# Twelve instead of eight tiles turned by VectorE, a ring of eight row slots, and loads reordered on SyncE's queue

## The chip, the cores and the metric

The kernel runs on one core of a Trainium2 chip. The metric is the time of one execution in device microseconds; the number given for the kernel before is the median of three runs.

## The reference, cut to what matters

2048 tokens of 512 values go through two layers. The first gives each token to one of four experts by its token id; the expert's matrix is `ctx_2048[e]`, used three times. The second is a gated MLP with 1408 inner columns, whose weights are -1, 0 or 1.

```python
def _L0_xattn_ref(hidden_states, token_ids, Wg, Wu, Wd):
    tid = jnp.clip(token_ids, 0, VOCAB - 1)
    expert_ids = jnp.minimum(tid // tokens_per_expert, E - 1)
    out = jnp.zeros_like(hidden_states)
    for e in range(E):
        g = jax.nn.silu(jnp.einsum('bsd,fd->bsf', hidden_states, Wg[e]))
        u = jnp.einsum('bsd,fd->bsf', hidden_states, Wu[e])
        y = jnp.einsum('bsf,df->bsd', g * u, Wd[e])
        out = jnp.where((expert_ids == e)[..., None], y, out)
    return out
...
    g = jnp.einsum('th,ih->ti', xf, gate_w) * gate_s
    u = jnp.einsum('th,ih->ti', xf, up_w) * up_s
    hdn = jax.nn.silu(g) * u
    out = jnp.einsum('ti,hi->th', hdn, down_w) * down_s
...
x = x + jnp.tanh(g_xattn[0]) * _L0_xattn_ref(_layernorm(x, axis=-1), itok, ctx_2048, ctx_2048, ctx_2048)
x = x + jnp.tanh(g_ffn[0]) * _L0_ffn_ref(_layernorm(x, axis=-1), gate_w, up_w, down_w, gate_s, up_s, down_s)
```

## The kernel before

**Stages.** First a routing stage sorts the tokens by expert into 19 tiles of 128 rows (16 full tiles of tokens, and up to three more because each expert starts a new tile). Then 19 steps of the expert layer, one for each tile (k = 0 to 18). Then four blocks of the MLP, each of four tiles. The order on every engine is written out by hand; engines meet through semaphores only.

**A step on TensorE** (`expert_step(k)`) is: `first_product(k)`, 12 matmuls of 128x512; while k+1 is under `ON_PE`, `turn_x(k + 1)`, four 128x128 transposes of the normalised rows of the next tile; `second_product(k - 1)`, again 12 matmuls; `turn_h(k)`, four transposes. `second_product(k - 1)` waits until `update(k - 2)` has emptied its PSUM bank (`rows_ready`) and for `h_lo(k - 1)`; `turn_h(k)` waits for `hidden(k)`.

**The rows of x.** GpSimd gathers a tile's rows from HBM into a ring slot (`gather`) and, after `update` on VectorE has added the expert's result, scatters them to HBM (`store`). The ring has `RING = 6` slots in the buffer `rows`, which has four more for the first MLP block. `stats(m)` is three VectorE instructions (bn_stats, bn_aggr, and the variance plus eps); GpSimd makes of them 1/std (`inverse_std`), and `norm(m)` writes the normalised rows into the one buffer `xn`.

**Turning x.** Of tiles 0 to 10 x is turned by TensorE. For tiles 11 to 18 SyncE writes `xn` to HBM (`turned_rows<-xn`), waits for it to land, and reads it back in another order (`xq<-turned_rows`): that is `turn_rows(n)` for tile n + 11. A VectorE transpose of 32x32 blocks (`turn`) then finishes it, and `turned_hi` (ScalarE) and `turned_lo` (VectorE) split it into the two parts that the matmuls take. The MLP blocks 1 to 3 turn their tiles in the same way.

**SyncE's queue** carries, in one order, the MLP's gate and up weights (`weight_row`, 8 rows of 704 KB), rows of the down weights only to be looked at (`check_row`, 11 of 256 KB), the pairs of write and read of `turn_rows`, and `load_half`, which brings two finished tiles (528 KB) from HBM back for MLP block 0. SyncE executes in order: a wait ahead of one of them holds all that follow. `first_stats(t)`, t = 0 to 3, are the statistics of these four tiles on VectorE; `first_stats(0)` waits for the first half and `first_stats(2)` for the second.

**Where the numbers are.** In the profile's lines: L1178 is either product of a step, L1157 `turn_x`, L1193 `turn_h`, L763 to L770 `stats`, L784 `norm`, L790 to L794 `first_stats`, L808 and L848 the low part of x, L822 `hidden`, L826 `h_lo`, L833 `update`, L842 the VectorE transpose, L535 `silu`, L339 and L344 write and read of `turn_rows`, L327 `load_half`, L306 `check_row`, L299 `weight_row`, L1283 and L1290 the MLP's matmuls.

Of the kernel before, what the change touches and what calls it, by code (L numbers as in the profile page):

```python
# [13 lines left out]
F32 = mybir.dt.float32  # L14
# [9 lines left out]
P = 128  # L24
# [15 lines left out]
RING = 6  # L40
ROWS = RING + BLOCK
# [13 lines left out]
ON_PE = 11  # L55
# [11 lines left out]
def ring_slot(k):  # L67

    return (k + 4) % RING


def row_slot(b, t):

    return t + RING * ((b + 1) % 2)

# [6 lines left out]
def build(nc, x, ids, ctxT, g_x, g_f, guT, dwT, gate_s, up_s, down_s, out):  # L82
# [7 lines left out]
    with ExitStack() as ctx:  # L90
# [12 lines left out]
        work = sb("work", [P, CTX_WORDS + XBUF_WORDS], F32R)  # L103
# [42 lines left out]
        xt0 = nc.alloc_sbuf_tensor_at("xt0", [P, D], F32, offset=work_base + (CTX_WORDS + 3 * D) * 4)  # L146
        wraw = nc.alloc_sbuf_tensor_at("wraw", [P, 2 * KC, 2, INTER], F32, offset=wgu_base)
# [65 lines left out]
        def token_of(first, last):  # L213

            return rows[:, first:last, D:D + 1].bitcast(U32)
# [30 lines left out]
        def quarter_rows(expert=False):  # L246

            return xq0[:, :] if expert else rows[:, RING - 2, 0:D]

        def turned_x(expert=False):  # L250

            return xt0[:, :] if expert else rows[:, RING - 1, 0:D]

# [3 lines left out]
        def down_w(c, s):  # L257
# [3 lines left out]
            row_landed w_hi w_lo down_hi down_lo  stored rows_a rows_b  # L261
# [9 lines left out]
        down_landed = [sem(f"down_landed{n}") for n in range(4)]  # L271
        last_stored = [sem(f"last_stored{t}") for t in range(BLOCK)]

# [7 lines left out]
        def _(sp):  # L281
# [36 lines left out]
            check_row(4)  # L318
            weight_row(4)
            sp.wait_ge(S["ctx_lo"], len(ON_VECTOR))  # L320
            sp.wait_ge(S["pool_ctx_lo"], len(ON_POOL))
            def load_half(b, half_):
                t = BLOCK * b + 2 * half_
                at = row_slot(b, 2 * half_)
                if b == 0:
                    sp.wait_ge(S["stored"], 16 * (t + 2 + EXPERTS - 1))
# [3 lines left out]
            for r in range(5, 2 * KC):  # L330
                check_row(r)
                weight_row(r)
            load_half(0, 0)
            check_row(8)

            def turn_rows(n):
# [3 lines left out]
                             xn[:, :].rearrange("p (i c) -> p i c", i=QUADS)).then_inc(S["xn_out"], 16)  # L340
# [5 lines left out]

            turn_rows(0)
            load_half(0, 1)
            check_row(9)
            turn_rows(1)  # L350
            check_row(10)
            for n in range(2, AHEAD):
                turn_rows(n)
            for c in range(IC):
                if c < 4:
                    sp.wait_ge(S["stored"], 16 * (TILES + c))
                else:
                    sp.wait_ge(S["down_lo"], c - 3)
# [14 lines left out]
        def _(pool):  # L373
# [30 lines left out]
            def gather(k):  # L404
                at = ring_slot(k)
                pool.indirect_dma_start(  # L406
                    rows[:, at, 0:D], None, x, bass.IndirectOffsetOnAxis(ap=gidx[:, k:k + 1], axis=0))\
                    .then_inc(slot_landed[at], 16)

            def store(k):  # L410
                pool.indirect_dma_start(  # L411
                    scratch, bass.IndirectOffsetOnAxis(ap=sidx[:, k:k + 1], axis=0),
                    rows[:, ring_slot(k), :], None).then_inc(S["stored"], 16)
# [8 lines left out]
            def token_in(k, count=1):  # L422
                at = ring_slot(k)
                pool.tensor_copy(token_of(at, at + count), gidx[:, k:k + count].unsqueeze(2))\
# [7 lines left out]
            def first_inverse_std():  # L432
# [7 lines left out]
                rows[0:16, ring_slot(5), 0:D], None, x,  # L440
                bass.IndirectOffsetOnAxis(ap=inow[0:16, 0:1], axis=0)).then_inc(S["early_row"], 16)
            pool.memset(rows[:, 0:RING, D:WIDE], 0.0).then_inc(S["pads"], 1)
# [7 lines left out]
            pool.wait_ge(S["pads"], 1)  # L450
            token_in(0, 2)
            token_in(2, 4)
# [949 lines left out]
```

## Time and profile before

| | |
|---|---|
| median of three runs | 386.21 us (384.73 to 387.35) |
| the profiled execution | 384.71 us, span 382.6 us |
| TensorE matmul busy | 364.2 us, 95% of the span |
| VectorE busy | 244.6 us, 64% |
| ScalarE / GpSimd busy | 147.5 us, 39% / 92.5 us, 24% |
| chain that ended last | TensorE 85%, VectorE 6%, DMA 5%, issue 2%, GpSimd 1% |
| granted TensorE clock | 0.997 of full speed |
| DMA | 45.39 MB, mean 119 GB/s |

A busy share is a mean over stages. The expert steps run from 22 us to about 135 us of the span, the MLP blocks from there to the end. The chain of waits names what was last at each moment, the timeline of an engine gives start, duration and, in brackets, the idle time before an instruction and what ended it. Start to start of two neighbours in a timeline is what an instruction takes of its engine; its own duration overlaps the next one a little.

### The profile page before, as it was taken

How to read it: one execution, taken by the hardware profiler on the slowest of the kernel's cores; microseconds unless marked ns; L12 is line 12 of the kernel's file. 1: busy time of each engine (PE TensorE's matmuls, PEld its weight loads, DVE VectorE, ACT ScalarE, POOL GpSimd, SP SyncE). 2: the span in 40 equal slices, each digit the busy share in tenths (PEclk: the TensorE clock that was granted, in tenths of full speed). 3: DMA queues.
4: the chain of work that ended last, by engine and by line, in shares of the span. 5: the costliest groups of instructions: out<-in, count | busy, mean ns of one | idle time of the engine just before them, and what ended most of it. 6: DMA issues, size and time to landing. Idle time of an engine off the chain costs nothing.

```text
span 382.6 us, 5569 instructions
## 1 busy us (share of the span) xinstructions
PE 364.2 (95%) x1704; PEld 298.0 (78%) x1704; DVE 244.6 (64%) x451; ACT 147.5 (39%) x266; POOL 92.5 (24%) x131
## 2 busy tenths in 40 slices
PE   3899999997999999999999999999999999999993
PEld 2478888786888878888888888888888888888892
DVE  6877666767998878779856256647346757323353
ACT  3466565646654536323322222322222322222230
POOL 7497454343461220011003110002201001300022
PEclk9999999999999999999999999999999999999998
DMA  6768876756654246432301412301232310200002
GB/s 224 274 217 259 260 275 195 261 142 222 218 165 142 84 140 192 140 86 57 82 0 55 169 55 83 82 0 55 76 119 69 95 27 27 82 0 0 0 29 86
DMA packets 27281, 45.39 MB, mean 119 GB/s; under 512 B 2928, under 2 KB 13168, under 8 KB 27264
## 3 DMA queue, kind: packets, MB, share of 16 engines
q1 hardware_dynamic: 22912, 30.83, 25.8%
q0 software_dynamic: 4352, 14.35, 10.4%
q8 instruction: 9, 0.15, 0.2%
q14 instruction: 8, 0.07, 0.1%
HBM read 30.59 MB, written 14.57 MB: 118 GB/s over the span
## 4 chain that ended last, share of the span: by engine, by line
PE 85%; DVE 6%; DMA 5%; issue 2%; POOL 1%; SPq 0%; ACT 0%; DVEq 0%; POOLq 0%
PE bank L1283 41%; PE bank L1178 21%; PE bank L1290 20%; DMA turned_rows<-xn 2%; PE bank L1193 2%; DMA rows<-x,gidx 2%; PE bank L1157 1%; DMA xq<-turned_rows 1%; PE bank L1147 0%; DVE rows L1060 0%; DMA ids_i<-ids 0%; DVE tmp L1053 0%; DVE parts L808 0%; DVE bn L763 0%; DVE xn L1053 0%
## 5 line engine op out<-in xcount | busy, mean ns | idle before, releaser
L1283 PE MATMUL bank<-work,wgu 128*128 (+1 forms) x736 | 167.3, 380 | 0.1
L1283 PEld LDWEIGHTS bank<-work,wgu 128*128 128x128 f32 x736 | 133.9, 188 | 27.1 <-issue 0.5
L1178 PE MATMUL bank<-work,parts 128*128 (+1 forms) x432 | 106.3, 397 | 2.0 <-ACT parts L522 1.7
L1178 PEld LDWEIGHTS bank<-work,parts 128*128 128x128 f32 x432 | 79.0, 188 | 18.8 <-issue 2.4
L1290 PE MATMUL bank<-work,hp 128*128 128x512 f32 x352 | 87.3, 390 | 0.2 <-DVE hp L1019 0.2
L1290 PEld LDWEIGHTS bank<-work,hp 128*128 128x128 f32 x352 | 65.7, 188 | 14.4 <-DVE hp L1019 0.6
L1000 DVE SCALAR_TENSOR_TENSOR sh<-bank,gs,sh 128x512 f32<-128x512 f32 x42 | 31.5, 749 | 55.4 <-PE bank L1283 55.4
L630 ACT ACTIVATE hp<-sh 128x512 fp32r<-128x512 f32 x42 | 26.6, 632 | 78.5 <-DVE sh L1000 78.5
L625 ACT ACTIVATE sh<-bank,gs 128x512 f32<-128x512 f32 x42 | 28.9, 688 | 72.0 <-PE bank L1283 71.2
L496 POOL DMA_INDIRECT out<-rows x16 | 16.2, 1011 | 128.3 <-DVE rows L1060 105.8
L1006 DVE TENSOR_TENSOR hp<-sh,hp 128x512 fp32r<-128x512 f32 x42 | 29.0, 691 | 22.3 <-ACT hp L630 22.3
L429 POOL TENSOR_TENSOR rstd<-ve,half 128x1 f32<-128x1 f32 x31 | 17.5, 564 | 104.4 <-DVE ve L770 104.2
L411 POOL DMA_INDIRECT x_rows<-rows,sidx x19 | 19.5, 1028 | 28.3 <-DVE rows L833 21.0
L406 POOL DMA_INDIRECT rows<-x,gidx x19 | 20.0, 1052 | 23.9 <-DMA x_rows<-rows,sidx 20.6
L763 DVE BATCH_NORM_STATS2 bn<-rows 128x6 f32<-128x512 f32 (+1 forms) x31 | 21.2, 684 | 0.8 <-DMA rows<-x,gidx 0.6
L531 ACT ACTIVATE parts<-bank 128x512 fp32r<-128x512 f32 x19 | 11.3, 596 | 25.0 <-PE bank L1193 22.5
L833 DVE SCALAR_TENSOR_TENSOR rows<-bank,tg,rows 128x512 f32<-128x512 f32 x19 | 14.2, 748 | 9.4 <-PE bank L1178 9.4
L822 DVE TENSOR_TENSOR sh<-bank,sh 128x512 f32<-128x512 f32 x19 | 13.1, 689 | 6.9 <-ACT sh L535 6.8
L535 ACT ACTIVATE sh<-bank 128x512 f32<-128x512 f32 x19 | 11.4, 598 | 12.5 <-PE bank L1178 11.1
L1043 DVE TENSOR_TENSOR work<-rows,work 128x512 f32 (+1 forms) x12 | 8.3, 692 | 9.7 <-ACT work L526 9.7
L826 DVE TENSOR_TENSOR parts<-bank,parts 128x512 fp32r<-128x512 f32 x19 | 13.0, 685 | 2.0 <-ACT parts L531 1.7
L842 DVE STREAM_TRANSPOSE rows<-rows 128x512 f32<-128x512 f32 x12 | 13.4, 1117 | 0.0
(134 smaller groups left out, 267.8 us busy)
## 6 DMA issues: line engine op xcount, KB each, us to landing
wraw<-guT SPq DMA_DIRECT2D x8, 704.0 KB
turned_rows<-xn SPq DMA_DIRECT2D x20, 256.0 KB
rows<-x_rows SPq DMA_DIRECT2D x8, 528.0 KB, 4.5
ctx_in<-ctxT SPq DMA_DIRECT2D x4, 1024.0 KB, 5.5
rows<-turned_rows SPq DMA_DIRECT2D x12, 256.0 KB
checked<-dwT SPq DMA_DIRECT2D x11, 256.0 KB
rows<-dwT SPq DMA_DIRECT2D x11, 256.0 KB, 2.8
xq<-turned_rows SPq DMA_DIRECT2D x8, 256.0 KB
```

The lines of the kernel that those rows point to most:

```text
L406: pool.indirect_dma_start(rows[:, at, 0:D], None, x, bass.IndirectOffsetOnAxis(ap=gidx[:, k:k + 1], axis=0))\
L411: pool.indirect_dma_start(scratch, bass.IndirectOffsetOnAxis(ap=sidx[:, k:k + 1], axis=0), rows[:, ring_slot(k), :], None).then_inc(S["sto ...
L429: pool.tensor_tensor(rstd[:, 0:1], ve[:, 0:1], half[:, :], ALU.pow)\
L496: pool.indirect_dma_start(out, bass.IndirectOffsetOnAxis(ap=token_of(row_slot(b, t), row_slot(b, t) + 1)[:, 0, :], axis=0), rows[:, row_sl ...
L625: act.activation(sh[:, :], g_ps[:, :], ACT.Silu, scale=gs[:, 0, c:c + 1])\
L630: act.activation(hslot(c)[:, 0, :], sh[:, :], ACT.Copy).then_inc(S["hhi_ready"], 1)
L763: dve.bn_stats(bn[:, 0, :], rows[:, ds(at, 1), 0:D]).then_inc(S["bn_parts"], 1)
L1000: dve.scalar_tensor_tensor(out=sh[:, :], in0=u_ps[:, :], scalar=gs[:, 1, c:c + 1], in1=sh[:, :], op0=ALU.mult, op1=ALU.mult).then_inc(S["h ...
L1006: dve.tensor_tensor(hslot(c)[:, 1, :], sh[:, :], hslot(c)[:, 0, :].bitcast(F32), ALU.subtract).then_inc(S["hlo_ready"], 1)
L1178: mm = pe.matmul(out_ps[:, :], part(s)[:, c * P:(c + 1) * P], ctx_w(e, c, w), start=n == 0, stop=n == last)
L1283: mm = pe.matmul(out_ps[:, tiles.start * P:tiles.stop * P], wgu[:, row + h, w, c * P:(c + 1) * P], moving, start=n == 0, stop=n == last)
L1290: mm = pe.matmul(acc_ps[u][:, :], hslot(c)[:, s, u * P:(u + 1) * P], down_w(c, w), start=c == 0 and n == 0, stop=c == IC - 1 and n == len( ...
```

## The change

`ON_PE` goes from 11 to 7, so VectorE turns x of tiles 7 to 18 and TensorE x of tiles 0 to 6. The ring gets eight slots: six in `rows` (`NEAR`), two in a new buffer `far`. The normalised rows of the tiles that VectorE turns get a buffer of their own, `xn_q`, and `norm(k + 3)` stands near the end of step k, where `norm(k + 2)` stood at the start of step k. `gather` runs five tiles ahead, not four. `store` counts in two semaphores by turns. On SyncE the later weight rows, the check rows and the two `load_half` are put among the `turn_rows`. The four `first_stats` stand in steps 10, 11, 12 and 13, each ahead of that step's `update`; before, two stood in front of step 9 and one each behind steps 11 and 13.

```diff
-RING = 6
-ROWS = RING + BLOCK
+RING = 8
+NEAR = 6
+ROWS = NEAR + BLOCK
...
-ON_PE = 11
+ON_PE = 7
...
+        xn_q = nc.alloc_sbuf_tensor_at("xn_q", [P, D], F32, offset=work_base + CTX_WORDS * 4)
+        far = nc.alloc_sbuf_tensor_at("far", [P, RING - NEAR, WIDE], F32,
+                                      offset=work_base + (CTX_WORDS + 6 * D) * 4)
...
-            check_row(4)
-            weight_row(4)
-            sp.wait_ge(S["ctx_lo"], len(ON_VECTOR))
-            sp.wait_ge(S["pool_ctx_lo"], len(ON_POOL))
...
-            for r in range(5, 2 * KC):
-                check_row(r)
-                weight_row(r)
-            load_half(0, 0)
-            check_row(8)
-
-            def turn_rows(n):
+            def turn_rows(n, between=None):
 
                 sp.wait_ge(S["xn_ready"], n + ON_PE + 1)
                 sp.dma_start(turned[n].rearrange("i p c -> p i c"),
-                             xn[:, :].rearrange("p (i c) -> p i c", i=QUADS)).then_inc(S["xn_out"], 16)
+                             (xn_q if n < AHEAD else xn)[:, :].rearrange("p (i c) -> p i c", i=QUADS))\
+                  .then_inc(S["xn_out"], 16)
+                if between is not None:
+                    check_row(between)
                 sp.wait_ge(S["xn_out"], 16 * (n + 1))
                 if n:
                     sp.wait_ge(S["xt_ready"], n)
                 sp.dma_start(quarter_rows(n < AHEAD),
                              turned[n].rearrange("i (a g) c -> (i a) (g c)", g=QUADS)).then_inc(S["xq_in"], 16)
 
-            turn_rows(0)
-            load_half(0, 1)
-            check_row(9)
-            turn_rows(1)
-            check_row(10)
-            for n in range(2, AHEAD):
-                turn_rows(n)
+            turn_rows(0, 4)
+            sp.wait_ge(S["ctx_lo"], len(ON_VECTOR))
+            sp.wait_ge(S["pool_ctx_lo"], len(ON_POOL))
+            for n in range(1, AHEAD):
+                turn_rows(n, n + 3 if 2 <= n < IC - 3 else None)
+                if n % 2 == 0 and n <= 8:
+                    weight_row(n // 2 + 3)
+                if n in (5, 7):
+                    load_half(0, (n - 5) // 2)
...
+            gather(6)
+            token_in(6)
             for k in range(2, STEPS + 1):
-                if k < ON_PE:
+                if k <= ON_PE - 3:
                     inverse_std(k + 2)
+                if ON_PE - 3 <= k < STEPS - 3:
+                    inverse_std(k + 3)
...
-                pool.wait_ge(S["stored"], 16 * (k - 1))
-                if k + 4 < STEPS:
-                    gather(k + 4)
-                    token_in(k + 4)
...
+                if k > 2:
+                    pool.wait_ge(*tile_stored(k - 3))
+                if k + 5 < STEPS:
+                    gather(k + 5)
+                    token_in(k + 5)
...
-            def step(k):
+
+            def step(k, block_row=None):
                 h_lo(k - 1)
-                if k + 2 < STEPS:
-                    norm(k + 2, ring_slot(k + 2))
-                if k + 1 > ON_PE:
-                    turn(k + 1 - ON_PE, True)
-                hidden(k)
-                if k + 1 == ON_PE:
-                    turn(0, True)
+                turn(k + 1 - ON_PE, True)
                 if k + 3 < STEPS:
                     landed(k + 3)
-                    begin_stats(ring_slot(k + 3))
+                    stats(k + 3, ring_rows(k + 3)[:, :, 0:D])
+                hidden(k)
                 turned_lo(k + 1)
                 if k + 3 < STEPS:
-                    end_stats(k + 3)
+                    norm(k + 3)
+                if block_row is not None:
+                    first_stats(block_row)
                 update(k - 1)
...
-            first_stats(0)
-            first_stats(1)
             last_on_pe(ON_PE - 2)
-            for k in range(ON_PE - 1, NORM_AT):
-                step(k)
-                if k % 2:
-                    first_stats((k - STATS_AT) // 2 + 2)
+            for k in range(ON_PE - 1, 14):
+                step(k, k - STATS_AT if k >= STATS_AT else None)
```

**On VectorE, one turned step.** These rows are step 11 of the kernel before, from `norm(13)` to `first_stats(2)`.

```order
L784 TENSOR_SCALAR xn<-rows,mv,rstd 128x4x4x32 [waits xn_out,rstd_ready]
L842 STREAM_TRANSPOSE xt_55<-xq_54 128x4x128 [waits xlo_ready,xq_in]
L822 TENSOR_TENSOR sh<-bank,sh 128x512 [waits silu_ready]
L763 BN_STATS bn<-rows 128x6 [waits slot_landed0]
L848 TENSOR_TENSOR parts<-xt_55,parts 128x512 [waits xhi_ready]
L768 BN_AGGR mv<-bn 128x2 [waits bn_parts]
L770 TENSOR_SCALAR ve<-mv 128x1 [waits bn_mv]
L833 SCALAR_TENSOR_TENSOR rows<-bank,tg,rows 128x512 [waits y_done]
L790 BN_STATS bn<-rows 128x6 [waits rows_b]
L792 BN_AGGR mv<-bn 128x2 [waits bn0_parts]
L794 TENSOR_SCALAR ve<-mv 128x1 [waits bn0_mv]
```

The step that answers to it, step 10 of the changed kernel, from `h_lo(9)` to `update(9)`:

```order
L845 TENSOR_TENSOR parts<-bank,parts 128x512 [waits hhi_ready]
L860 STREAM_TRANSPOSE xt_55<-xq_54 128x4x128 [waits xlo_ready,xq_in]
L782 BN_STATS bn<-far 128x6 [waits slot_landed7]
L787 BN_AGGR mv<-bn 128x2 [waits bn_parts]
L789 TENSOR_SCALAR ve<-mv 128x1 [waits bn_mv]
L841 TENSOR_TENSOR sh<-bank,sh 128x512 [waits silu_ready]
L866 TENSOR_TENSOR parts<-xt_55,parts 128x512 [waits xhi_ready]
L803 TENSOR_SCALAR xn_q<-far,mv,rstd 128x4x4x32 [waits xn_out,rstd_ready]
L809 BN_STATS bn<-rows 128x6 [waits rows_a]
L811 BN_AGGR mv<-bn 128x2 [waits bn0_parts]
L813 TENSOR_SCALAR ve<-mv 128x1 [waits bn0_mv]
L852 SCALAR_TENSOR_TENSOR rows<-bank,tg,rows 128x512 [waits y_done]
```

The transpose now stands ahead of the statistics, the norm behind `turned_lo`, and `first_stats` (L809 to L813, with its wait for `rows_a`) between the norm and `update` (L852).

**On SyncE, around the first two loads of finished rows.** These rows are of the kernel before, from `check_row(7)` and `weight_row(7)` to the read of tile 12, with the pairs of tiles 11 and 12 and both loads.

```order
L306 DMA checked<-dwT 128x512 [waits checks_done,check_landed]
L299 DMA wraw<-guT 128x1408 [waits row_landed]
L327 DMA rows<-x_rows 128x2x528 [waits stored]
L306 DMA checked<-dwT 128x512 [waits checks_done,check_landed]
L339 DMA turned_rows<-xn 128x4x128 [waits xn_ready]
L344 DMA xq_54<-turned_rows 128x512 [waits xn_out]
L327 DMA rows<-x_rows 128x2x528 [waits stored]
L306 DMA checked<-dwT 128x512 [waits checks_done,check_landed]
L339 DMA turned_rows<-xn 128x4x128 [waits xn_ready]
L344 DMA xq_54<-turned_rows 128x512 [waits xt_ready,xn_out]
```

These are of the changed kernel, from the write of tile 12 (n = 5) to the second `load_half`.

```order
L349 DMA turned_rows<-xn_q 128x4x128 [waits xn_ready]
L324 DMA checked<-dwT 128x512 [waits checks_done,check_landed]
L357 DMA xq_54<-turned_rows 128x512 [waits xt_ready,xn_out]
L343 DMA rows<-x_rows 128x2x528 [waits stored0,stored1]
L349 DMA turned_rows<-xn_q 128x4x128 [waits xn_ready]
L324 DMA checked<-dwT 128x512 [waits checks_done,check_landed]
L357 DMA xq_54<-turned_rows 128x512 [waits xt_ready,xn_out]
L317 DMA wraw<-guT 128x1408 [waits row_landed]
L349 DMA turned_rows<-xn_q 128x4x128 [waits xn_ready]
L324 DMA checked<-dwT 128x512 [waits checks_done,check_landed]
L357 DMA xq_54<-turned_rows 128x512 [waits xt_ready,xn_out]
L343 DMA rows<-x_rows 128x2x528 [waits stored0,stored1]
```

Each `load_half` (L327, now L343) now stands behind a write of `xn_q`, the wait for its landing, and the read; before, the first stood ahead of all writes, and the second between the pair of tile 11 and the pair of tile 12.

## Rows read from the trace of the kernel before

**Rows 1.** The page, section 1: busy us, share of the span, instructions.

```profile
PE 364.2 (95%) x1704; PEld 298.0 (78%) x1704; DVE 244.6 (64%) x451; ACT 147.5 (39%) x266; POOL 92.5 (24%) x131
```

**Rows 2.** The chain of waits: start us, duration us, what, steps 7, 8, 13, 14.

```profile
60.02 2.77 PE bank L1178 x12
...
66.43 2.77 PE bank L1178 x12
...
100.67 5.47 PE bank L1178 x24
...
106.58 5.49 PE bank L1178 x24
```

**Rows 3.** Timeline of TensorE: start, duration, line, operation, idle before it.

```profile
76.30 0.66 PE L1157 MATMUL bank<-ident,xn 128*128 128x128 f32 x4 [0.70 <-DVE xn L784]
...
87.77 5.75 PE L1178 MATMUL bank<-work,parts 128*128 x24 [1.66 <-ACT parts L522]
...
94.53 5.71 PE L1178 MATMUL bank<-work,parts 128*128 x24 [0.28 <-issue]
```

**Rows 4.** Timeline of VectorE, steps 9 to 11.

```profile
73.10 0.68 DVE L790 BATCH_NORM_STATS2 bn<-rows 128x6 f32<-128x512 f32 x1
...
75.11 0.68 DVE L826 TENSOR_TENSOR parts<-bank,parts 128x512 fp32r<-128x512 f32 x1
...
80.45 0.68 DVE L763 BATCH_NORM_STATS2 bn<-rows 128x6 f32<-128x512 f32 x1
...
81.57 0.68 DVE L826 TENSOR_TENSOR parts<-bank,parts 128x512 fp32r<-128x512 f32 x1
...
91.92 1.10 DVE L842 STREAM_TRANSPOSE xt<-xq 128x512 f32<-128x512 f32 x1 [1.89 <-DMA xq<-turned_rows]
92.86 0.68 DVE L822 TENSOR_TENSOR sh<-bank,sh 128x512 f32<-128x512 f32 x1
```

**Rows 5.** Timeline of VectorE, steps 13 and 14.

```profile
100.70 0.74 DVE L833 SCALAR_TENSOR_TENSOR rows<-bank,tg,rows 128x512 f32<-128x512 f32 x1
101.36 0.68 DVE L826 TENSOR_TENSOR parts<-bank,parts 128x512 fp32r<-128x512 f32 x1
101.95 0.54 DVE L784 TENSOR_SCALAR xn<-rows,mv,rstd 128x512 f32<-128x512 f32 x1
...
104.09 0.69 DVE L822 TENSOR_TENSOR sh<-bank,sh 128x512 f32<-128x512 f32 x1
104.70 0.69 DVE L763 BATCH_NORM_STATS2 bn<-rows 128x6 f32<-128x512 f32 x1
...
106.18 0.75 DVE L833 SCALAR_TENSOR_TENSOR rows<-bank,tg,rows 128x512 f32<-128x512 f32 x1
```

**Rows 6.** Timeline of SyncE's queue: turning pairs and the second load of finished rows.

```profile
79.04 0.38 SPq L339 DMA_DIRECT2D turned_rows<-xn  x1
82.89 0.33 SPq L344 DMA_DIRECT2D xq<-turned_rows  x1
83.26 0.45 SPq L327 DMA_DIRECT2D rows<-x_rows  x1
...
84.26 0.43 SPq L339 DMA_DIRECT2D turned_rows<-xn  x1
89.16 0.32 SPq L344 DMA_DIRECT2D xq<-turned_rows  x1
...
120.91 0.37 SPq L339 DMA_DIRECT2D turned_rows<-xn  x1
123.36 0.32 SPq L344 DMA_DIRECT2D xq<-turned_rows  x1
```

**Rows 7.** DMA issues of window 65:66 us: issues, KB, us to landing.

```profile
rows<-x_rows SPq DMA_DIRECT2D x1, 528.0 KB, 6.3
```

**Rows 8.** DMA issues, window 83:83.8 us.

```profile
rows<-x_rows SPq DMA_DIRECT2D x1, 528.0 KB, 4.5
```

**Rows 9.** DMA issues, window 215:217 us, in the MLP.

```profile
rows<-x_rows SPq DMA_DIRECT2D x2, 528.0 KB, 4.1
```

More of the change, by code:

```diff
@@ L211, in token_half, with ring_rows, ring_row, token_of @@
             return slice(i * D // 2, (i + 1) * D // 2)
-        def token_of(first, last):
-            return rows[:, first:last, D:D + 1].bitcast(U32)
+        def ring_rows(k, count=1):
+            at = ring_slot(k)
+            return rows[:, at:at + count, :] if at < NEAR else far[:, at - NEAR:at - NEAR + count, :]
+        def ring_row(k):
+            return ring_rows(k)[:, 0, 0:D]
+        def token_of(b, t):
+            return rows[:, row_slot(b, t), D:D + 1].bitcast(U32)
         def first_xt(i):
@@ L246, in quarter_rows @@
         def quarter_rows(expert=False):
-            return xq0[:, :] if expert else rows[:, RING - 2, 0:D]
+            return xq0[:, :] if expert else rows[:, NEAR - 2, 0:D]
         def turned_x(expert=False):
-            return xt0[:, :] if expert else rows[:, RING - 1, 0:D]
+            return xt0[:, :] if expert else rows[:, NEAR - 1, 0:D]
         def ctx_w(e, c, s):
@@ L260, in build @@
         names = """ids_in small_in consts route_pe route_sb route_step tables_ready low_ready first_ready
-            row_landed w_hi w_lo down_hi down_lo  stored rows_a rows_b
+            row_landed w_hi w_lo down_hi down_lo rows_a rows_b
             bn_parts bn_mv var_ready rstd_ready xn_ready xt_done xhi_ready xlo_ready
@@ L271, in build, with tile_stored @@
         down_landed = [sem(f"down_landed{n}") for n in range(4)]
+        stored = [sem(f"stored{n}") for n in range(2)]
         last_stored = [sem(f"last_stored{t}") for t in range(BLOCK)]
+        def tile_stored(k):
+            return stored[k % 2], 16 * (k // 2 + 1)
         def hold(eng):
@@ L449, in _ @@
             gather(3)
[L450 to L452 removed]
+            pool.wait_ge(S["pads"], 2)
+            token_in(0, 4)
+            token_in(4, 2)
             inverse_std(1)
@@ L829, in update @@
             def update(k):
-                at = ring_slot(k)
+                row = ring_rows(k)[:, :, 0:D]
                 dve.wait_ge(S["y_done"], k + 1)
-                dve.scalar_tensor_tensor(out=rows[:, ds(at, 1), 0:D], in0=y_ps[:, :].unsqueeze(1),
-                                         scalar=tg[:, 0:1], in1=rows[:, ds(at, 1), 0:D],
+                dve.scalar_tensor_tensor(out=row, in0=y_ps[:, :].unsqueeze(1), scalar=tg[:, 0:1], in1=row,
                                          op0=ALU.mult, op1=ALU.add).then_inc(S["rows_ready"], 1)
@@ L852, in step_on_pe @@
                 h_lo(k - 1)
-                norm(k + 1, ring_slot(k + 1))
+                norm(k + 1)
                 landed(k + 2)
-                stats(k + 2, ring_slot(k + 2))
+                stats(k + 2, ring_rows(k + 2)[:, :, 0:D])
                 hidden(k)
                 x_lo(k + 1)
+                if k == ON_PE - 3:
+                    norm(k + 2)
+                    landed(k + 3)
+                    stats(k + 3, ring_rows(k + 3)[:, :, 0:D])
                 update(k - 1)
@@ L929, in _ @@
             ctx_lo(6, 7)
-            norm(3, ring_slot(3))
+            norm(3)
             h_lo(1)
@@ L934, in _ @@
             landed(4)
-            stats(4, ring_slot(4))
+            stats(4, ring_rows(4)[:, :, 0:D])
             update(1)
-            norm(4, ring_slot(4))
+            norm(4)
             ctx_lo(7, 9)
```

77 lines of the change are left out of this document (38 added, 39 removed).

## The prediction

> **What bounds the kernel now.** I read the page first: TensorE is busy 95% of the span [rows 1], so time can only come from work taken off TensorE or from its stalls. The chain of waits says where the stalls are. In the expert layer it is TensorE for step after step. T(k) below is the start of `first_product(k)`. Step 7 starts at 60.02 and step 8 at 66.43 [rows 2]: a step in which TensorE also turns x takes 6.41 us. Step 13 starts at 100.67 and step 14 at 106.58: a step without `turn_x` takes 5.91 us. Between T(8) = 66.43 and T(13) = 100.67 lie 34.24 us, but the five steps need 2 x 6.41 + 3 x 5.91 = 30.55 us. So TensorE loses 3.7 us around the place where VectorE takes over the turning. TensorE's timeline shows where [rows 3]: 0.70 us for the norm of tile 10, 1.66 us for ScalarE's part of the first turned tile, 0.28 us in the next step, and the rest in short pieces that the timeline does not bracket.
>
> Who was late there? VectorE did two `first_stats` in a row, from 73.10 to 75.11, before `h_lo` and the norm [rows 4]; that is the first stall. Then it waited 1.89 us at 91.92 for the read-back of a turned tile [rows 4]: the norm ends at 79.04, the write takes until 82.89 (3.85 us), the next write until 89.16 (4.90 us) [rows 6]. From step 13 on TensorE runs without a gap.
>
> **Term 1: four transposes leave TensorE.** Steps 6 to 9 lose their `turn_x`: 4 x (6.41 - 5.91) = 2.0 us less, all of it on the path.
>
> **Term 2: the old stall at the switch.** The switch moves to steps 5 and 6, where no `first_stats` stand, and the norm leads by more than a step. I walk it by offsets. T(5) = 47.2 and T(6) = 53.6, one and two steps before 60.02 in round numbers. `norm(7)` starts behind `h_lo`, at T(5) + 0.69 + 0.59 (100.67, 101.36, 101.95 [rows 2, 5]), and ends at T(5) + 1.8; a write of 3.85 us lands at T(5) + 5.7; a read of 2.7 us (89.16 to 91.92 [rows 4, 6]) at T(5) + 8.4 = T(6) + 2.0. The transpose takes 0.94 (91.92 to 92.86), the statistics 1.12 (80.45 to 81.57) [rows 4], and `hidden` 0.61 (104.09 to 104.70) [rows 5]: done at T(6) + 4.7. `turn_h(6)` wants it at T(6) + 5.5, where the second product ends. So the whole 3.7 us go. With the 4.90 us write it would come 1.05 us later and cost 0.3 us at most. I take 0.
>
> In the steady state the norm ends at T(k) + 5.1 and the transpose is wanted at T(k+2) + 1.3, which is 8.0 us later; write and read need 3.85 + 2.7 = 6.6 us, 7.6 us with the longest write. It holds either way. Terms 1 and 2 together: -5.7 us.
>
> **What VectorE now has to do in a step.** Start to start: `update` 0.66, `h_lo` 0.59, transpose 0.94, statistics 1.12, `hidden` 0.61, low part of x 0.59 (as `h_lo`), norm 0.54 [rows 4, 5]. The sum is 5.05 us, under the 5.91 us of TensorE. A `first_stats` adds 1.0 (73.10 to 75.11 for two). Steps 10 to 13 each have one: 6.05 us, 0.14 more than a step. The fixed points are `hidden` at T + 3.42 (104.09) and `update` at T + 5.51 (106.18) [rows 5]; so the norm runs from T + 4.6 to T + 5.1. This lag alone stays within the slack.
>
> A page argues against this. The Trainium skill, "VectorE: DVE Perf Modes", section "Rules for kernel authors", says to use TensorE for a 128x128 transpose if PSUM is an acceptable destination. Its table has 311 ns for one on VectorE, so four per tile make 1.2 us, an estimate; by it steps 10 to 13 would each lag 0.3 us more, and the sum below would be 1.2 us higher. The trace has 0.94 us for a whole tile (91.92 to 92.86 [rows 4]), on the engine with 0.86 us to spare, against 0.50 us on the one with none, and I go by the trace.
>
> **Term 3: the two loads of finished rows, the new wait.** In step 10 VectorE stands at `first_stats(0)`, ahead of `update(9)`, until `load_half(0, 0)` has landed. That load is now queued on SyncE behind the write of tile 12, its landing, and the read. `norm(12)` ends at T(9) + 5.1 = T(10) - 0.8. Add w for the write, 0.37 for issuing the read (82.89 to 83.26 [rows 6]), and L for the load. Then the stall. Behind a `first_stats` that starts at T(11) + x come 1.0 + 0.66 + 0.59 + 0.94 + 1.12 + 0.61 = 4.92 us until `hidden(11)` is out, and `turn_h(11)` wants that at T(11) + 5.48 (the two products of 5.47 us, rows 2). So the stall is x - 0.56, and nothing when x is less.
>
> First pair: x = -0.8 + w + 0.37 + L - 5.91 = w + L - 6.3, stall w + L - 6.9. The second pair is worse. VectorE is by then held against its own chain: `hidden(11)` ends at the stall's end, so `norm(14)` ends 0.7 us into step 12. Step 12 costs another 0.14 us and is 6.05 us long. The load for `first_stats(2)` lands at 0.7 + w + 0.37 + L, so x = w + L - 5.0 and the stall w + L - 5.5. Steps 12 and 13 add 0.14 each. Together: 2(w + L) - 12.1 us.
>
> **w and L from rows.** w: 2.45 us for a late write (120.91 to 123.36), 3.85 us with a gather beside it, 4.90 us behind a load and a check row [rows 6]. In the change a check row (256 KB) follows the write at once, as much as a gather; I take 3.85. Below about 3.1 w saves nothing, because the read also waits for the previous tile's transpose. L: 4.1 us in the MLP, where two loads go together (1056 KB) [rows 9], 4.5 us at 83.26 [rows 8], 6.3 us at 65.44 behind weights [rows 7]. Here the load shares its time with the read and a gather, 528 + 256 + 256 KB, which is nearest to the 4.1 us. So w + L = 7.95 and term 3 is 3.8 us (1.05 + 2.45 + 0.28).
>
> The Trainium skill, "DMA: Bandwidth & Descriptors", section "Anatomy of one DMA — SWDGE (gpsimd) path", gives 2.0 us and bytes over 436 GB/s, for another issuing path. An estimate from it: 3.2 us for the 528 KB load, and term 3 of about 1.7 us with a 3.1 us write. No row here has a load of this size under 4.1 us.
>
> **Edits at nothing.** Weight rows 4 to 7, now issued behind the reads of n = 2, 4, 6 and 8 in steps 7, 9, 11 and 13, are first used in steps 10, 12, 14 and 16; that cover of three steps is 17 us, and without it ScalarE would wait. A check row is issued 0.8 us before the step that uses it and wanted behind `silu` and `turned_hi`, about 4 us into it, so it may take 4.8 us. GpSimd's `gather(6)` and its copy now precede `inverse_std(4)`; `turn_x(4)` wants that norm only behind a product of 2.77 us [rows 2], so 0, and at most some tenths. Gathers come a step earlier and find a free slot. In the MLP TensorE has no gap to fill, and nothing there changes but the first down loads, which have slack.
>
> **Sum.** -2.0 - 3.7 + 3.8 = -1.9, on 384.71 us: 382.8 us. The median shown is 1.5 us above the profiled execution, so I forecast 384.3 us. A change under 1% (3.9 us) cannot be told from none here.
>
> **The rivals.** (1) *The loads come in time.* The pair of 1056 KB lands in 4.1 us [rows 9]; if all of that were moving, one load alone would take 2.05 us, which is the floor of L; I take 2.8, nearer to it than to 4.1. With w at its floor of 3.1 the first stall goes and the second is 0.4: term 3 is under 1 us and the gain 4.8 us: 381.4 us, down to 380.5 with no stall. For it: the write and read of late tiles are quick (2.45 us). Against: in steps 10 to 12 weight rows 5 and 6 go out behind the reads of n = 4 and 6 and run into just these writes. 25%. (2) *The loads come very late.* The wait for `rows_a` and `rows_b` takes the place of the old stall and exceeds it. With the longest rows, w = 4.9 and L = 6.3, term 3 is 10.3 us: 384.71 - 5.7 + 10.3 = 389.3, or 390.8 us on the median. It is break-even at w + L = 8.9 and over 1% slower from 10.8. For it: DMA carries four more write-read pairs in the same stretch, and both longest rows come from stretches with a weight row or a load in flight. Against: both must be at their worst twice. 10%. (3) *The turning chain stays late in each step*, because the write crosses weight and check rows: 7.6 us of 8.0 leaves 0.4, and a write of 5.5 would cost 0.2 us in each of twelve steps, 2.4 us. That gives 386.7 us, within 1%. 7%. The forecast itself: 58%.
>
> **Range and chances.** The forecast's own range, w + L from 7.2 to 8.8, is 382.8 to 386.0 us. To hold 8 in 10 it must reach into rival 1 and towards rival 2: 381.0 to 388.4. Faster by over 1% is rival 1 and a little of the forecast, 0.27; within 1% is the rest of it and rival 3, 0.62; slower 0.11.
>
> **What would show it.** In the profile after: 16 matmuls fewer on the line of `turn_x`, and steps 6 to 9 of 5.9 us; no stall of TensorE between T(5) and T(10); VectorE idle ahead of `first_stats(0)` and `first_stats(2)`, ended by the loads, some 2 us each; TensorE stalls at `turn_h(11)` and `turn_h(13)` of 1.0 and 2.5 us. I am wrong if VectorE never waits for those loads, if `turn` waits for its read in most steps, or if TensorE stalls at the switch again.

## The result: slower by 2.3%, and the profile after

| | before | changed |
|---|---|---|
| median | 385.94 us (4 runs, 384.73 to 387.35) | 394.69 us (4 runs, 394.18 to 395.96) |
| the profiled execution | 384.71 us, span 382.6 us | 394.89 us, span 392.8 us |
| granted TensorE clock | 0.997 | 0.991 |

The ratio is 1.023, with a 95% interval of 1.0187 to 1.0274. Ratios here and below compare fast executions only, because some executions of the same kernel take over 1.5% longer than its fastest. Forecast were 384.3 us and "within 1%"; the time lies above the range of 381.0 to 388.4 us. Between the two profiled executions are 10.2 us, and I account for these.

The page of the changed kernel, section 1, answers to [rows 1]:

```profile
PE 372.0 (95%) x1688; PEld 298.5 (76%) x1688; DVE 248.2 (63%) x455; ACT 148.1 (38%) x266; POOL 95.6 (24%) x132
```

TensorE has the 16 matmuls less that were to go, and is busy 7.8 us longer. That is the first sign of something that no wait explains. The MLP stage starts at 139.69 us instead of 135.53, 4.16 us later, and from there to the end of the span it takes 253.1 instead of 247.1 us. So 6.0 us of the loss lie in a stage where the change adds no instruction to TensorE and where it has no gap. The chain of waits in that stage, first of the kernel before, then of the changed one (start, duration, what):

```profile
199.56 3.63 PE bank L1283 x16
203.18 1.81 PE bank L1290 x8
205.00 3.63 PE bank L1283 x16
208.62 1.81 PE bank L1290 x8
```

```profile
197.76 1.86 PE bank L1303 x8
199.62 3.72 PE bank L1296 x16
203.34 1.82 PE bank L1303 x8
205.16 3.73 PE bank L1296 x16
208.89 1.86 PE bank L1303 x8
```

The groups are the same, each stands close behind the one before it, and all but one are longer: 3.73 for 3.63 us, 1.86 for 1.81. It is not the clock, as the row of windows of the changed kernel says (stretch, length, busy time and count of TensorE, its weight loads, VectorE, ScalarE, GpSimd, then the granted clock, DMA share, GB/s):

```profile
200.00:260.00 60.00, 60.00 (x260) 48.69 (x259) 32.56 (x55) 16.32 (x25) 6.31 (x8) 1.00 0.23 71
```

The clock is granted in full (2.4 GHz). One matmul of 512 columns takes 5.58/24 = 232 ns instead of 5.44/24 = 227 ns. And one group is not slow: at 203.34 the down product takes 1.82 us. So does every eleventh of them. Of the two operands of a matmul, the stationary one (128x128) is a block of `wgu`, `parts` or `hp`, and the moving one (128x512) lies in `work` in all these products. The quick down products are the ones whose stationary operand `hp[2]` lies inside `work` too; the other two `hp` buffers, `wgu` and `parts` lie behind `work`, and the changed kernel has made `work` 32 words (128 bytes) longer. That pointed at addresses. 44 chunks x 0.135 us make 5.9 of the 6.0 us.

In the expert layer the products are slower too. The chain of waits there names the read of the first turned tile, the two products of a step, and the two pairs of a write and the load queued behind it:

```profile
52.94 5.14 DMA xq<-turned_rows
...
68.02 5.58 PE bank L1191 x24
...
79.27 4.96 DMA turned_rows<-xn_q
...
84.66 5.30 DMA rows<-x_rows
...
96.02 3.84 DMA turned_rows<-xn_q
...
100.29 3.86 DMA rows<-x_rows
...
116.38 5.58 PE bank L1191 x24
```

Where [rows 2] have 5.49 us for 24 matmuls there now are 5.58; a step is 6.02 us long instead of 5.91, some 1.7 us over the stage. The stalls stand in TensorE's timeline:

```profile
60.84 0.66 PE L1206 MATMUL bank<-ident,sh 128*128 128x128 f32 x4 [0.85 <-DVE sh L841]
...
92.08 4.50 PE L1191 MATMUL bank<-work,parts 128*128 x12 [3.21 <-DVE rows L852]
...
106.28 3.05 PE L1191 MATMUL bank<-work,parts 128*128 x12 [0.47 <-DVE rows L852]
```

and in VectorE's, with what ended each wait:

```profile
58.10 1.09 DVE L860 STREAM_TRANSPOSE xt<-xq 128x512 f32<-128x512 f32 x1 [2.33 <-DMA xq<-turned_rows]
...
89.99 0.69 DVE L809 BATCH_NORM_STATS2 bn<-rows 128x6 f32<-128x512 f32 x1 [4.72 <-DMA rows<-x_rows]
...
104.18 0.69 DVE L809 BATCH_NORM_STATS2 bn<-rows 128x6 f32<-128x512 f32 x1 [1.96 <-DMA rows<-x_rows]
```

The two waits of `first_stats` for a load are there, in the places forecast. They hold `update` (L852), for which TensorE waits at 92.08 and 106.28. The granted clock falls there, as a split of that stretch into windows shows:

```profile
88.00:92.00 4.00, 0.87 (x4) 0.38 (x2) 1.95 (x5) 0.88 (x3) 0.00 (x0) 0.99 0.64 227
92.00:96.40 4.40, 4.32 (x12) 3.41 (x13) 4.22 (x9) 1.24 (x3) 2.80 (x3) 0.62 0.53 171
96.40:98.00 1.60, 1.60 (x10) 1.38 (x9) 1.50 (x5) 0.93 (x2) 0.22 (x2) 1.00 1.01 382
```

Behind the idle time it is 0.62 in the mean, between its two levels of 1.2 and 2.4 GHz, and the 12 matmuls take 4.50 us; from 96.4 us it is full again. From T(10) = 80.05 to T(15) = 116.38 lie 36.3 us where five steps of 6.02 us take 30.1, so this stretch loses 6.2 us.

### The profile page after: what moved, and what is told of

The parts are those of the page before. It is cut to its first block, busy times and chain, and to the rows that moved or that the text cites. A ratio compares the mean times of both kernels' runs of the same rounds, so it can differ in the third digit from the quotient of the medians.

```text
span 392.8 us, 5551 instructions
## 1 busy us (share of the span) xinstructions
PE 372.0 (95%) x1688; PEld 298.5 (76%) x1688; DVE 248.2 (63%) x455; ACT 148.1 (38%) x266; POOL 95.6 (24%) x132
## 4 chain that ended last, share of the span: by engine, by line
PE 81%; DMA 10%; DVE 5%; issue 1%; ACT 1%; POOL 1%; SPq 0%; DVEq 0%; POOLq 0%
PE bank L1296 42%; PE bank L1303 20%; PE bank L1191 16%; DMA turned_rows<-xn_q 3%; DMA rows<-x_rows 2%; DMA rows<-x,gidx 2%; DMA ctx_in<-ctxT 1%; PE bank L1206 1%; DMA xq<-turned_rows 1%; ACT work L527 1%; DVE xt L860 1%; DVE sh L841 0%; PE bank L1160 0%; PE bank L1170 0%; DVE bn L782 0%
## 5 line engine op out<-in xcount | busy, mean ns | idle before, releaser
L1296 PE MATMUL bank<-work,wgu 128*128 (+1 forms) x736 | 171.1, 385 | 0.1
L1191 PE MATMUL bank<-work,parts 128*128 (+1 forms) x432 | 108.8, 404 | 4.6 <-DVE rows L852 3.7
L1191 PEld LDWEIGHTS bank<-work,parts 128*128 128x128 f32 x432 | 80.5, 191 | 24.0 <-issue 5.9
L1303 PE MATMUL bank<-work,hp 128*128 128x512 f32 x352 | 88.9, 394 | 0.2 <-DVE hp L1032 0.2
L425 POOL DMA_INDIRECT x_rows<-rows,sidx x15 | 15.4, 1027 | 35.7 <-DVE rows L852 34.6
L782 DVE BATCH_NORM_STATS2 bn<-rows 128x6 f32<-128x512 f32 (+1 forms) x27 | 18.1, 671 | 0.2 <-DMA rows<-x,gidx 0.2
L420 POOL DMA_INDIRECT rows<-x,gidx x15 | 17.1, 1143 | 3.8 <-issue 2.6
L860 DVE STREAM_TRANSPOSE xt<-xq 128x512 f32<-128x512 f32 x12 | 13.1, 1093 | 2.3 <-DMA xq<-turned_rows 2.3
L852 DVE SCALAR_TENSOR_TENSOR rows<-bank,tg,rows 128x512 f32<-128x512 f32 x15 | 11.2, 746 | 4.0 <-PE bank L1191 4.0
```

Of the source, the lines that this page charges most:

```text
L420: pool.indirect_dma_start(ring_row(k), None, x, bass.IndirectOffsetOnAxis(ap=gidx[:, k:k + 1], axis=0))\
L782: dve.bn_stats(bn[:, 0, :], row).then_inc(S["bn_parts"], 1)
L860: dve.transpose(turned_x(expert).rearrange("p (h a g) -> p g h a", h=KC, g=QUADS), quarter_rows(expert).rearrange(order, g=QUADS, h=KC))\
L1191: mm = pe.matmul(out_ps[:, :], part(s)[:, c * P:(c + 1) * P], ctx_w(e, c, w), start=n == 0, stop=n == last)
L1296: mm = pe.matmul(out_ps[:, tiles.start * P:tiles.stop * P], wgu[:, row + h, w, c * P:(c + 1) * P], moving, start=n == 0, stop=n == last)
L1303: mm = pe.matmul(acc_ps[u][:, :], hslot(c)[:, s, u * P:(u + 1) * P], down_w(c, w), start=c == 0 and n == 0, stop=c == IC - 1 and n == len( ...
```

## Experiments

Two questions: is it the address that makes the matmuls slow (theories A, S and G in the expectations), or some other traffic or the clock; and what the loads cost. Each ratio is to the kernel before on the same chip. Intervals are 95%; a row without one is a single run.

| run | median us (runs) | before | ratio |
|---|---|---|---|
| before, `work` + 128 bytes | 394.55 (4) | 385.70 | 1.020 [1.0125, 1.0272] |
| before, `work` + 256 bytes | 384.48 (1) | 385.83 | |
| before, `work` + 64 bytes | 393.52 (1) | 385.95 | |
| before, `work` + 32 bytes | 395.67 (1) | 385.95 | |
| before, gap behind `wgu` | 388.38 (1) | 385.83 | |
| before, gap ahead of `work` | 386.36 (1) | 385.83 | |
| changed, `work` as long as before | 389.82 (10) | 385.70 | 1.010 [1.0065, 1.0133] |
| changed, loads two tiles earlier | 390.95 (4) | 385.70 | 1.016 [1.0074, 1.0243] |
| changed, both | 387.66 (10) | 385.70 | 1.0025 [0.9985, 1.0065] |
| both, SyncE's order rewritten | 383.48 (10) | 385.83 | 0.997 [0.9923, 1.0012] |
| the same with nine tiles on TensorE | 381.60 (5) | 385.95 | 0.986 [0.9811, 0.9913] |

### The shift alone, in the kernel before

```diff
-        work = sb("work", [P, CTX_WORDS + XBUF_WORDS], F32R)
+        work = sb("work", [P, CTX_WORDS + XBUF_WORDS + 32], F32R)
```

> The kernel before with one edit: the buffer work is 32 words (128 bytes) longer per partition, as in the changed kernel, so that every buffer behind it (wgu, parts, rows) starts 128 bytes later; nothing uses the words. Theory A (where the stationary operand of a matmul starts in SBUF sets its pitch): the MLP's 24 matmuls of an inner chunk and a down product go from 5.44 us to 5.57 us, the MLP stage from 247 to about 253 us, the expert stage by 1 to 2 us more, in all 7 to 8 us slower, 393 to 394 us. Down products of the eleventh chunk, whose operand lies in work itself, stay at 1.81 us. Theory B (the slower matmuls come with the changed instruction streams, the drop of the clock or the chip of the day): no change, 385 to 387 us.

Nobody reads or writes the added words. 394.55 us (394.24 without the longest of the four runs): the kernel before becomes as slow as the changed one. Its chain in the MLP has the same pattern, one quick down product included:

```profile
265.11 3.72 PE bank L1283 x16
268.82 1.82 PE bank L1290 x8
270.65 3.73 PE bank L1283 x16
274.37 1.86 PE bank L1290 x8
```

From the first matmul of the MLP to the end of the span it takes 253.0 us, as in the changed kernel (253.1), against 247.1 us before. So all that the MLP lost comes from 128 bytes. (The granted clock of this trace is 0.83 from 20 to 40 us and from 80 to 100 us; the groups and the stage that are compared ran at 1.00.)

### The changed kernel without the shift

```diff
-        work = sb("work", [P, CTX_WORDS + XBUF_WORDS + 2 * (WIDE - D)], F32R)
+        work = sb("work", [P, CTX_WORDS + XBUF_WORDS], F32R)
...
-        spare = work_base + (CTX_WORDS + XBUF_WORDS // 2) * 4
+        spare = work_base + (CTX_WORDS + XBUF_WORDS // 2 - 32) * 4
...
+            act.wait_ge(*tile_stored(12))
             first_x_hi(0)
```

`xq0`, `xt0` and `far` move down by 32 words in the same way; the added wait keeps `first_x_hi(0)` off a ring slot still in use.

> The changed kernel with the 32 extra words taken back: far, xt0, xq0 and checked start 32 words earlier inside work, so that wgu, parts and rows start where they do in the kernel before. Everything else, orders and waits, as changed. Theory A: matmul pitch back to 5.44 us in the MLP, 7 to 8 us faster than the changed kernel, 386 to 388 us: what is left against before is the stall at the loads minus the transposes and the old stall. Theory B: stays at 394 to 395 us.

389.82 us, 4.9 us less than the changed kernel, and above the 386 to 388 us expected. The MLP's groups are back at 3.63 and 1.81 us, products of 24 at 5.49. The remaining 2.8 of the 7.7 us did not come back. This profile has longer stalls: TensorE idle 4.06 us (3.21 in the changed kernel) before the products behind `first_stats(0)`, the 12 matmuls after it in 5.48 us (4.50), and a start 0.5 us later. Whether the edit makes them longer, or they differ from run to run (the ten runs took 387.35 to 391.69 us), is not shown. Undoing the shift does not make the change a gain.

### The loads two tiles earlier, the shift left in

```diff
-                if n in (5, 7):
-                    load_half(0, (n - 5) // 2)
+                if n in (3, 5):
+                    load_half(0, (n - 3) // 2)
```

> The changed kernel with the two loads of finished rows issued two turning pairs earlier (behind the reads of n = 3 and n = 5 instead of 5 and 7); the buffers stay where the change put them. Theory L (the waits for these loads at first_stats(0) and first_stats(2) cost TensorE about 9 us in steps 10 to 13): VectorE no longer waits for them, TensorE stalls of steps 11 and 13 go, 6 to 9 us faster than the changed kernel, 386 to 389 us. Rival (the loads only moved a wait that the crowded DMA makes anyway, at the turning pairs): under 2 us faster, 393 to 394 us.

390.95 us, 3.7 us less than the changed kernel, where 6 to 9 us were expected. VectorE no longer waits at `first_stats`, and the MLP starts at 135.75, as early as before the change. The price shows on ScalarE, which waits for a check row that takes 8.03 us to land, and through it on TensorE (their timelines):

```profile
88.66 0.63 ACT L578 ACTIVATE down_junk<-checked 128x512 f16 x1 [4.61 <-DMA checked<-dwT]
...
90.31 3.05 PE L1191 MATMUL bank<-work,parts 128*128 x12 [1.42 <-ACT parts L549]
```

### Both

The edits of the last two together.

> Both edits on the changed kernel: buffers at their old addresses and the loads two pairs earlier. Theories A and L together: the two effects add, 378 to 381 us, faster than the kernel before by 1.3 to 2%. If one of them is wrong, 386 to 388 us; if both are, 393 us or more.

387.66 us: my 378 to 381 us was missed by 7 us. The two gains, 4.9 and 3.7 us, add to 8.6, and 7.0 came; so most of the miss lies in the two summands, each of which had come out smaller than expected when it was tried alone. What holds TensorE now is the turning itself. The chain of waits of this run goes from one write of a turned tile to the next, each with a check row issued behind it:

```profile
69.74 5.25 DMA turned_rows<-xn_q
...
75.91 5.83 DMA turned_rows<-xn_q
...
82.62 6.34 DMA turned_rows<-xn_q
...
89.82 5.52 DMA turned_rows<-xn_q
...
96.29 6.40 DMA turned_rows<-xn_q
```

The forecast took 3.85 us for a write and 4.90 for a slow one; a write of 5.5 us was the case of rival 3, the turning chain late in each step. TensorE idles 1.34 us at 63.35, 0.78 at 88.52 and 0.93 at 109.28, each time for `hidden`, which stood on VectorE behind a transpose that had waited for its read (2.73, 1.09 and 0.93 us), and 0.52 us at 105.34 for an `update` behind a norm that had waited 1.30 us for a write to land. The mean DMA share from 80 to 100 us is 0.90.

ScalarE waits for check rows here as well, which the prediction had costed "at nothing":

```profile
90.15 0.63 ACT L578 ACTIVATE down_junk<-checked 128x512 f16 x1 [2.61 <-DMA checked<-dwT]
...
103.66 0.63 ACT L578 ACTIVATE down_junk<-checked 128x512 f16 x1 [3.65 <-DMA checked<-dwT]
```

In this trace VectorE's waits for reads and writes end later than these, so what the check rows alone cost here is not shown; in the run with the earlier loads alone they cost the 1.42 us at 90.31.

### SyncE's order rewritten

This goes on top of both edits. Weight row 4 and check row 4 go ahead of the first pair, the other check rows one pair earlier, weight rows 5 to 7 behind pairs 2, 4 and 7, loads behind pairs 3 and 5. The stretch from 40 to 50 us has room in the changed kernel: its windows are

```profile
40.00:50.00 10.00, 10.00 (x51) 8.22 (x50) 8.25 (x19) 5.80 (x12) 5.24 (x8) 1.00 0.44 154
80.00:88.00 8.00, 8.00 (x39) 6.50 (x37) 4.66 (x9) 5.89 (x11) 3.22 (x4) 1.00 0.94 299
88.00:98.00 10.00, 6.79 (x25) 5.17 (x24) 7.67 (x17) 3.05 (x8) 3.02 (x4) 0.83 0.65 227
```

a DMA share of 0.44 at 40 to 50 us and 0.94 at 80 to 88 us, where the first write-load pair falls. The kernel before has 0.83 at 40 to 50 us.

```diff
-            turn_rows(0, 4)
             sp.wait_ge(S["ctx_lo"], len(ON_VECTOR))
             sp.wait_ge(S["pool_ctx_lo"], len(ON_POOL))
+            weight_row(4)
+            check_row(4)
+            turn_rows(0)
             for n in range(1, AHEAD):
-                turn_rows(n, n + 3 if 2 <= n < IC - 3 else None)
-                if n % 2 == 0 and n <= 8:
-                    weight_row(n // 2 + 3)
-                if n in (5, 7):
-                    load_half(0, (n - 5) // 2)
+                turn_rows(n, n + 4 if n < IC - 4 else None)
+                if n in (2, 4, 7):
+                    weight_row({2: 5, 4: 6, 7: 7}[n])
+                if n in (3, 5):
+                    load_half(0, (n - 3) // 2)
```

> The changed kernel at the old addresses (as the second run), the loads of finished rows two pairs earlier (as the fourth), and SyncE's order loosened: weight row 4 and check row 4 ahead of the first turning pair, each later check row one pair earlier, weight rows 5 to 7 behind the reads of n = 2, 4 and 7. Theory D (what the fourth run still loses, some 5 us of stalls in steps 6 to 12, are check rows, reads and writes that land late because SyncE's reads and checks crowd into 70 to 110 us while the DMA engines idle from 40 to 50 us): ScalarE's waits for check rows fall from 2 to 4 us each to under 1, stalls of TensorE between steps 6 and 12 fall under 2 us, total 381 to 384 us. Rival (the DMA engines are simply full in that stretch: the order does not matter): within 1 us of the fourth run, 387 to 388 us.

383.48 us, 4.2 us less than the run before it in the table. Against the kernel before the interval still includes 1, and it overlaps a little with that of the run before; seven of the ten runs took 382.54 to 384.38 us, three 387.31 to 388.06. ScalarE's waits for check rows in the expert layer are gone. The writes are not quick (one takes 5.98 us at 73.14), and the DMA share from 80 to 100 us is still 0.88. What is left is the turning chain: TensorE idles 0.23 us at the switch and 1.13 us at 85.71, where VectorE's `hidden` was late.

### Which addresses matter

Five more edits of the kernel before, each run once. The kernel before itself varies by some us from run to run (384.70 to 391.30 in these sessions), so the groups of matmuls and the length of the MLP stage say more here than the total. `work` longer by 64 words (256 bytes):

> The kernel before with work 64 words (256 bytes) longer, nothing else. If the slower pitch comes from operands that start 128 bytes off a 256-byte grid, the chunk is at 5.44 us and the time at 385 to 387 us. If it comes from being off a 512-byte grid or from any shift against the moving operand, the chunk is at 5.57 us and the time about 393 us.

384.48 us, groups of 3.63 and 1.81 us, the MLP stage 247.7 us. A longer `work` is harmless at 256 bytes.

A gap of 32 words behind `wgu`, ahead of `parts`:

```diff
         parts_base = nc.sbuf_base
+        gap_words = sb("gap_words", [P, 32], F32)
         parts = sb("parts", [P, 4, D], F32R)
```

> The kernel before with a gap of 32 words between wgu and parts: parts (x and h of the expert layer, and two of the three h buffers of the MLP) and all behind it shift by 128 bytes, work and wgu stay. Theory S (it is the stationary operand's start): expert products go from 2.77 to 2.80 us for 12, the MLP's down products (8 matmuls) from 1.81 to 1.86 except in every eleventh chunk, gate and up products (16 matmuls) stay at 3.63; about 2 us slower than before plus some 1 to 2 us of the expert stage, 388 to 390 us. Rival (it is wgu alone, or the sum of all): all pitches as before, or all slower.

388.38 us. The expectation for the down products missed, by my edit: `parts_base` is taken ahead of the gap, and `hp[0]` and `hp[1]`, which are placed by it, did not move; only `parts` did. Read with that, the run separates the two stages. In its chain an expert step, whose `parts` moved, is slow (5.48 us in the kernel before), and the MLP, unmoved, is quick:

```profile
109.80 5.58 PE bank L1179 x24
...
203.16 3.63 PE bank L1284 x16
...
206.79 1.81 PE bank L1291 x8
```

The same gap ahead of `work`, so that all buffers behind move together:

```diff
+        gap_words = sb("gap_words", [P, 32], F32)
         work_base = (nc.sbuf_base + 31) // 32 * 32
```

> The kernel before with a gap of 32 words ahead of work: stationary and moving operands all shift by 128 bytes together. Theory S with an absolute grid: all pitches slow, the eleventh chunk's down product too (1.86 us for 8), 393 to 395 us. Rival, a clash of the two operands' relative places: all pitches as before, 385 to 387 us.

386.36 us, the MLP stage 247.2 us, and the groups are quick:

```profile
201.34 3.63 PE bank L1284 x16
204.97 1.81 PE bank L1291 x8
```

So a common shift of both operands by 128 bytes does nothing; what matters is where one stands relative to the other. In the kernel before, the lengths of the buffers put every stationary operand a multiple of 512 bytes from its moving one. `work` longer by 16 words (64 bytes) and by 8 words (32 bytes):

> The kernel before with work 16 words (64 bytes) longer. Shifting the stationary operands by 128 bytes against the moving one slowed the pitch by 2.4%, shifting both together did not, nor did 256 bytes. Theory G (what counts is the difference of the two starts modulo 256): 64 bytes is off too, chunk at 5.57 us or something between, 389 to 394 us. Rival (only a difference of exactly 128 clashes): 5.44 us, 385 to 387 us.

> The kernel before with work 8 words (32 bytes) longer. Theory G: slower pitch than 5.44 us, 388 us or more. Rival: 5.44 us, 385 to 387 us.

393.52 and 395.67 us; the chain of the 64-byte kernel has

```profile
203.15 3.73 PE bank L1283 x16
206.89 1.87 PE bank L1290 x8
```

and that of the 32-byte one the same 3.73 and 1.87. The MLP stage takes 254.1 and 254.3 us, with 128 bytes 253.0, against 247.1 in the kernel before. Steps of 32, 64 and 128 bytes are all slow, by 2.5 to 3%. What the engine does in these 5 ns per matmul, no run shows, and no distance above 256 bytes or below 32 was tried.

### Nine tiles on TensorE

The kernel with SyncE's order rewritten, and `ON_PE` 9. VectorE turns ten tiles, the switch comes two steps later, and weight rows 4 and 5, check rows 4 to 6 and the first load go ahead of the first pair. The rest of the order moves with them.

```diff
-ON_PE = 7
+ON_PE = 9
...
+            weight_row(4)
+            check_row(4)
+            weight_row(5)
+            check_row(5)
+            load_half(0, 0)
+            check_row(6)
+            turn_rows(0)
```

> The seventh variant of the order: the changed kernel at the old addresses, with ON_PE = 9 (TensorE turns x of tiles 0 to 8, VectorE of 9 to 18), weight rows 4 and 5, check rows 4 to 6 and the first load of finished rows ahead of the first turning pair, the second load behind the read of n = 2, weight rows 6 and 7 behind n = 1 and 4, each check row as early as its buffer is free. Against the fifth run it takes two turning pairs (1 MB) out of the crowded stretch for 1.0 us more of transposes. Theory D (late landings in 70 to 100 us are what is left): stalls fall by 2 us, 381 to 383 us, and fewer runs at 387 us. Rival (the DMA engines were no longer the cause, only the transposes count): 1 us slower than the fifth run, 384 to 385 us.

381.6 us, ratio 0.986 [0.9811, 0.9913]: the only kernel here whose interval lies below 1, by 1.4%. Its trace is of the slowest of the five runs (385.50 us, the other four 380.92 to 381.72), with a late start (the MLP at 135.79), and so does not show where the gain lies. In its TensorE timeline from the switch on one larger stall is left:

```profile
93.83 0.65 PE L1213 MATMUL bank<-ident,sh 128*128 128x128 f32 x4 [1.05 <-DVE sh L848]
```

It gives up two of the four saved `turn_x`, 1.0 us, and gets two turning pairs less in the crowded stretch and a first load ahead of all pairs. The second load (79.75) still meets a write (80.69), which takes 6.01 us and leads to the stall above. The number of tiles and the order were changed together, and no run separates them.

## Why the prediction was wrong, by its steps

**The failed step is "Edits at nothing".** Its last sentence, "In the MLP TensorE has no gap to fill, and nothing there changes", was wrong: the MLP took 253.1 us instead of 247.1. That is 6.0 of the 10.2 us; with the 1.7 us of the expert layer the shift cost 7.7 us. I read the diff for instructions and waits, and the line that made `work` 32 words longer has none. The padded kernels before show it: 8.8, 7.6 and 9.7 us more with 128, 64 and 32 bytes and no other edit. The shift was the largest part of the miss and not the only one: terms 2 and 3 were too small by 4.0 us together.

**Term 1 was right.** Steps 7 to 9 run without `turn_x`, and a step is 6.02 us, which is 5.91 and the shift.

**Term 2 was mis-sized.** The switch was to be free; it costs 1.6 us in all (0.85 at 60.84, 0.23 behind it, the rest in short pieces: from the start of step 6 to that of step 8 are 13.61 us, where two steps take 12.04). I had taken 2.7 us for the read of the first turned tile, and it took 5.14 us. A slow write of 4.90 us was in my bounds, a slow read was not. A stall at the switch was one of my own signs of being wrong.

**Term 3 was mis-sized; its wait was right, the split and the place of the stall were not.** The formula was 2(w + L) - 12.1 with w + L = 7.95. Measured are w = 4.96 and L = 5.30 at the first, 3.84 and 3.86 at the second: w + L = 10.3 and 7.7. Put into the forecast's formulas they give a first stall of 10.3 - 6.9 = 3.4 us (TensorE idle 3.21), a second of 7.7 - 5.5 = 2.2, and with the 0.3 us for lag 5.9 us; measured are 6.2. But I had TensorE stall at `turn_h(11)` and `turn_h(13)`, for `hidden`. It stalls half a step earlier, at the second products, which wait for the `update` right behind `first_stats`; I had left that wait out. And behind the second load TensorE idles only 0.47 us and 0.27 at 110.10, while behind the first the 12 matmuls last 4.50 us instead of 2.80, 1.7 us that no term held. The two belong together, as the rows suggest: `norm(14)` ended at 96.0, about 1.0 us before step 12 began, where I had it 0.7 us behind, because TensorE was 1.7 us late by its clock; so the second load was 1.7 us less late for TensorE, and 2.2 - 1.7 = 0.5 us is what it idled. No run tests this. That the sum came close in spite of a clock that I had not counted is luck.

The rows that should have warned me are the second write of [rows 6], behind a load and a check row, with 4.90 us where I took 3.85, and the load at 65.44, with 6.3 us [rows 7]. The forecast chose the quiet rows for a stretch that was to carry more. (The 1.7 us that the prediction gives as term 3 for a load of 3.2 us and a write of 3.1 does not follow from its formulas, which make 1.1 us of it; nothing rests on it.)

**Check rows** were costed at nothing with a bound of 4.8 us. ScalarE waited 0.57 to 1.38 us for them in the changed kernel, and up to 4.61 us once the loads came earlier.

**The steps added up.** Start 0.35 and a short wait in step 3 0.2 (neither traced to its cause), switch 1.6, loads 6.2, slower products in the expert layer 1.7, less 2.0 and 3.7: 4.3 us, measured 4.16; with 6.0 in the MLP 10.3 us, measured 10.2. From the forecast's -1.9 us the gap is 12.1: the shift 7.7, loads 2.4, switch 1.6, start and step 3 0.5, which is 0.1 us too much.

**The rivals.** Rival 2, the late loads (10%), came nearest in place, with w + L = 10.3 in the first pair only. Rivals 1 and 3 did not occur in the changed kernel; rival 3 came once the loads were earlier. None of them held the shift. Without the shift this kernel took 389.82 us: with the loads and the switch alone it is above the upper end of the range (388.4 us) as well.

## What to carry to other kernels

A diff moves addresses as well as instructions: where a buffer changes its length, ask what lies behind it and which matmul reads one operand on either side of it, and keep the distance between the two as it was; 256 bytes more did no harm here, 32, 64 and 128 did. When an engine that never waits becomes slower in a stage that was not edited, compare the same group of instructions in both chains before looking for a wait. And where a DMA chain is moved into a stretch, take its durations from rows of equal load, the longest of them, the read as well as the write, and find room for the transfers around it where the DMA share is low, as the rewritten order did (4.2 us between the medians).

## What the runs showed of the hardware

- The same 128x512 matmul takes 227 or 232 ns in the MLP by the relative start of its stationary and moving operands: quick at the old distance, at 256 bytes more and when both move by 128 bytes together, 2.5 to 3% slower at 32, 64 and 128 bytes more. On a kernel that is 95% matmul that is 8 to 10 us of 386. The Trainium skill, "SBUF — State Buffer", section "Operand start alignment", asks only that an operand start at a multiple of its element size, and says that this is about legality, not speed; all the starts here meet it, and the speeds differ.
- Behind an idle time of TensorE of 3.21 us the granted clock was 0.62 in the mean over 4.4 us, and 12 matmuls took 4.50 us instead of 2.80. In the kernel without the shift they took 5.48 us behind 4.06 us of idle, at a granted clock of 0.50, the lower level of 1.2 GHz.
- Writes and reads of 256 KB in the turning took 2.5 to 6.4 us, the longest in the run with a DMA share of 0.90 around them; the 528 KB load took 3.9 to 6.3 us, and one check row of 256 KB 8.03 us.
